# A recurrence with a mixture of experts: the shared experts' activations turned by DMA instead of TensorE

## The reference

```python
x = x + wkv(w, u, layernorm(x), ctx)        # a recurrence over the 128 tokens of each sample
n = layernorm(x)                            # (2048 tokens, 512)
p, sel = top_k(softmax(n @ gate_w.T), 2)    # 8 routed experts, two of them per token
routed = sum_e p_e * (silu(n @ G_e.T) * (n @ U_e.T)) @ D_e.T      # inner size 256
shared = (silu(n @ Gs.T) * (n @ Us.T)) @ Ds.T                     # inner size 1024
x = x + routed + sigmoid(n @ gs.T) * shared
```

## Time and profile before

| | us |
|---|---|
| time, median of 3 runs | 565.46 (563.67 to 566.19) |
| time of the profiled execution | 566.06 |
| its span, first to last instruction | 564.3 |
| TensorE busy | 486.2 (86% of the span) |
| VectorE busy | 421.3 (75%) |
| POOL busy | 345.4 (61%) |
| ScalarE busy | 275.9 (49%) |

### The profile page before, as it was taken

One profiled execution on the slowest core, in us unless ns is written; L12 is line 12 of the kernel. 1 busy time (PEld: TensorE's weight loads), 2 busy tenths in 40 slices (PEclk: granted clock), 3 DMA queues, 4 the chain that ended last, 5 costly groups with the idle time before them and its releaser, 6 DMA issues.

```text
span 564.3 us, 10142 instructions
## 1 busy us (share of the span) xinstructions
PE 486.2 (86%) x2671; PEld 258.5 (46%) x2671; DVE 421.3 (75%) x954; ACT 275.9 (49%) x534; POOL 345.4 (61%) x422
## 2 busy tenths in 40 slices
PE   1116789899999999999999979999999999999970
PEld 1113345345455555454555435445545555555530
DVE  5678987899989899999898867566656656666650
ACT  4848837575573864765837333433333333333310
POOL 5767956857948669588486364334375565555332
PEclk9999989999999999999999999999999999999995
DMA  7970105105213223151101320315576776677453
GB/s 283 415 271 19 38 19 187 57 21 188 76 46 143 77 82 143 38 188 62 52 20 39 105 88 15 113 45 102 101 122 117 141 119 116 110 131 123 69 73 38
DMA packets 25929, 59.14 MB, mean 105 GB/s; under 512 B 6314, under 2 KB 6314, under 8 KB 24338
## 3 DMA queue, kind: packets, MB, share of 16 engines
q0 software_dynamic: 9824, 20.90, 21.3%
q1 hardware_dynamic: 16050, 37.59, 18.5%
HBM read 37.83 MB, written 20.65 MB: 104 GB/s over the span
## 4 chain that ended last, share of the span: by engine, by line
PE 52%; POOL 17%; issue 10%; DVE 9%; DMA 7%; ACT 3%; SPq 1%; POOLq 0%; DVEq 0%; ACTq 0%
PE GU L884 28%; PE DN L899 14%; DMA out<-wall,idsa 5%; POOL wall L445 4%; PE XT L829 3%; PE HT L829 3%; POOL yb L429 2%; POOL nrm L411 2%; POOL nrm L413 2%; DVE wall L1071 2%; POOL wall L424 2%; POOL wall L421 2%; DVE wall L1078 1%; PE YT L829 1%; SPq L366 1%
## 5 line engine op out<-in xcount | busy, mean ns | idle before, releaser
L884 PE MATMUL GU<-wall,xt 128*128 128x512 f16 x768 | 187.0, 384 | 2.1 <-DVE wall L1173 2.0
L899 PE MATMUL DN<-wall,hx 128*128 128x512 f16 (+1 forms) x618 | 150.8, 380 | 7.2 <-DVE hx L1200 4.5
L884 PEld LDWEIGHTS GU<-wall,xt 128*128 128x128 f16 x768 | 74.8, 99 | 70.4 <-issue 3.7
L584 POOL DMA_INDIRECT out<-wall,idsa x39 | 62.0, 1590 | 73.1 <-SPq L370 35.1
L659 ACT ACTIVATE hx<-HT 128x256 f16<-128x256 f32 x103 | 39.0, 379 | 127.4 <-PE HT L829 110.6
L899 PEld LDWEIGHTS DN<-wall,hx 128*128 128x128 f16 x618 | 60.4, 98 | 81.9 <-issue 6.0
L1200 DVE TENSOR_TENSOR hx<-HT,hx 128x256 f16<-128x256 f32 x103 | 43.1, 418 | 64.3 <-ACT hx L659 59.7
L654 ACT ACTIVATE th<-GU,scl 128x256 f32<-128x256 f32 x103 | 48.5, 471 | 80.0 <-PE GU L884 76.1
L884 PE MATMUL GU<-wall,kb 128*128 x240 | 61.4, 379 | 0.2 <-DVE kb L1374 0.2
L884 PE MATMUL GU<-wall,xnb 128*128 x228 | 58.5, 379 | 0.6 <-DVE xnb L1374 0.6
L574 POOL DMA_INDIRECT xb<-xn_rows,idsi x39 | 40.2, 1030 | 30.5 <-DMA out<-xb 16.3
(11 more groups left out here) (163 smaller groups left out, 747.3 us busy)
## 6 DMA issues: line engine op xcount, KB each, us to landing
wall<-wgu SPq DMA_DIRECT2D x12, 1024.0 KB, 9.7
wall<-wd SPq DMA_DIRECT2D x12, 512.0 KB, 10.3
out<-xb SPq DMA_DIRECT2D x20, 256.0 KB
xb<-x SPq DMA_DIRECT2D x16, 256.0 KB, 2.7
cb<-ctx_t SPq DMA_DIRECT2D x16, 256.0 KB
xn_rows<-xnb SPq DMA_DIRECT2D x16, 256.0 KB
xb<-xn_rows,idsi POOLq DMA_INDIRECT x39
out<-wall,idsa POOLq DMA_INDIRECT x39
```

What stands on the lines that cost most here:

```text
L584: pool.indirect_dma_start(out, bass.IndirectOffsetOnAxis(ap=idsa[:, j:j + 1], axis=0), ye[j % RESULTS], None, compute_op=ALU.add).then_inc ...
L884: ins = nc.tensor.matmul(GU[par][:], lhs(xp, c), gate_up(base, wp, c), start=m == 0, stop=m == 3 * HC - 1)
L899: ins = nc.tensor.matmul(DN[:], hx[par][:, hp * IE + c * P:hp * IE + (c + 1) * P], down(base, wp, c), start=start and m == 0, stop=stop an ...
```

## The change

The 64 shared units' activations are no longer transposed on TensorE. `unit_hi` and `hidden_lo` now work on hb itself and leave both f16 halves in row layout in a new buffer hr (two of them); SP then issues one transposing DMA for each unit (`turn_hidden`), hr (128 x 512, f16) into hx, of which there are now three. The down products of every unit, routed ones too, come three units behind (HX = 3) instead of two. The routed units keep their transposes on TensorE, into bank YT instead of HT. The accumulate of the sums moves later in VectorE's lists: in a turn from behind hidden_lo(n) to behind hidden(n+2), likewise in the two blocks of shared units, and accumulate(15) from expert unit 1 to expert unit 2. hidden_lo(n) moves ahead of first_stats. The weights of a routed expert are loaded in six DMAs of 256 KB, spread over two turns and placed between the transposing DMAs, and some loads of x come a turn later. After the last routed unit stand its transposes and then three down products. One of the two hb buffers is now the bank HB (the former HT). Some small buffers share memory with others.

```diff
 GUW, DW = HC * 2 * IE, IC * H
 UW = GUW + DW
 LAG = 2
+HX = 3
+PIECES = 6
 NX = LAG + 1
 NB = 6
 SPLIT0 = 1
...
 
         KT, YT, XT, LG = bank("KT"), bank("YT"), bank("XT"), bank("LG")
         GU = [bank("GU0"), bank("GU1")]
-        HT, DN = bank("HT"), bank("DN")
+        HB, DN = bank("HB"), bank("DN")
+        hb = [HB[:, 0:IE], hb1[:, :]]
+        hb_routed = [by_time[:, 0:IE], hb1[:, :]]
 
 
         small_ld, x_ld, c_ld, e_ld = sems("small_ld x_ld c_ld e_ld")
...
                 sp.dma_start(xn_dram[first * P:last * P, H:XW].rearrange("(t p) e -> p t e", p=P),
                              r_d[:, first * E:last * E].rearrange("p (t e) -> p t e", e=E)).then_inc(probs_st, 16)
 
-            def load_expert(e):
-                base = (e + 1) * UW
-                wait_from(sp, e_ld, e * 32)
-                if e >= 2:
-                    sp.wait_ge(sh_gu_lo, SU)
-                    sp.wait_ge(sh_d_lo, SU)
-                src = (wgu[e], wd[e]) if isinstance(e, int) else tuple(
-                    w[ds(e, 1), :, :].rearrange("a p n -> (a p) n") for w in (wgu, wd))
-                sp.dma_start(span(wall, base, GUW), src[0]).then_inc(e_ld, 16)
-                sp.dma_start(span(wall, base + GUW, DW), src[1]).then_inc(e_ld, 16)
+            def load_expert(e, first=0, last=PIECES):
+
+                base, n = (e + 1) * UW, UW // PIECES
+                if first == 0:
+                    wait_from(sp, e_ld, e * PIECES * 16)
+                    if e >= 2:
+                        sp.wait_ge(sh_gu_lo, SU)
+                        sp.wait_ge(sh_d_lo, SU)
+                for k in range(first, last):
+                    src = wgu[e][:, k * n:(k + 1) * n] if k * n < GUW else wd[e][:, k * n - GUW:(k + 1) * n - GUW]
+                    sp.dma_start(span(wall, base + k * n, n), src).then_inc(e_ld, 16)
+
+            def turn_hidden(n):
+
+                sp.wait_ge(h_lo, n + 1)
+                wait_from(sp, dn, n - HX + 1)
+                sp.dma_start(hx[n % HX][:, :].rearrange("p (c t) -> p c t", t=P), hr[n % 2][:],
+                             transpose=True).then_inc(h_turned[n % HX], 16)
 
             sp.dma_start(wu_sb[:], wu).then_inc(small_ld, 16)
             sp.dma_start(wr_raw[:], wr).then_inc(small_ld, 16)
...
             sp.dma_start(ids_tiles[LISTS:LISTS + 1, :], pad_rows[0:1, :].bitcast(I32)).then_inc(ids_zst, 16)
             load_expert(0)
 
+            for i in range(LAG):
+                if i > 0:
+                    load_ctx(i + 1)
+                    load_expert(1)
+                    store_xn(i - 1)
+                load_x(i + 3)
+
             def turn(i, j, sq_e, hi_e, ws_e, lo_e):
-                if 0 < i < B - 1:
+                n = j * SU
+                due = squares_of(i + 1) if i + 1 in SQUARED_IN[2:] else squares_of(i + 2) if i + 2 in SQUARED_IN[2:] else None
+                k = PIECES // 2 if i + 1 in SQUARED_IN[2:] else 0
+
+                def piece(u):
+                    if due is not None:
+                        load_expert(due, k + u, k + u + 1)
+
+                if j > 0:
+                    turn_hidden(n - 1)
+                if i == LAG:
+                    load_x(i + 3)
+                if i > LAG + 1 and i + 2 < B:
+                    load_x(i + 2)
+                if i < B - 1:
                     load_ctx(i + 1)
-                if i == 1:
-                    load_expert(1)
-                if i + 1 in SQUARED_IN[2:]:
-                    load_expert(squares_of(i + 1))
-                if i > 0:
-                    store_xn(i - 1)
-                if j is not None and j > 0:
+                piece(0)
+                turn_hidden(n)
+                piece(1)
+                turn_hidden(n + 1)
+                store_xn(i - 1)
+                piece(2)
+                turn_hidden(n + 2)
+                if j > 0:
                     store_sum(j - 1)
-                if i + 3 < B:
-                    load_x(i + 3)
                 if i == B - 1:
                     store_probs(0, 0, PART)
 
-            turns(turn)
-
+            turns(turn, LAG)
+
+            n = SU * (B - LAG)
+            turn_hidden(n - 1)
             sp.wait_ge(y_rdy, B)
-            load_expert(E - 1)
+            load_expert(E - 1, 0, 3)
+            turn_hidden(n)
             store_xn(B - 1)
+            load_expert(E - 1, 3, 6)
+            turn_hidden(n + 1)
+            turn_hidden(n + 2)
             store_sum(B - LAG - 1)
 
+            turn_hidden(n + 3)
             store_probs(1, PART, B)
-            for j in range(B - LAG, B - 1):
-                store_sum(j)
+            for u in range(3):
+                turn_hidden(n + SU + u)
+            store_sum(B - 2)
+            turn_hidden(N_EXP - 1)
             store_sum(B - 1)
 
             sp.wait_ge(waits_rdy, WAIT_STEPS)
             for j in range(1, NSLOT):
-
 
                 for r in range(min(j, RESULTS)):
                     if j < RESULTS:
...
                 nc.scalar.activation(th[par][:], GU[par][:, 0:IE], ACT.Tanh, scale=scale(row, TANH)).then_inc(tanh, 1)
 
             def unit_hi(n, par):
-                act.wait_ge(h_t, n + 1)
-                wait_from(act, dn, n - 1)
-                nc.scalar.activation(hx[par][:, 0:IE], HT[:, 0:IE], ACT.Copy).then_inc(h_hi, 1)
+                if n >= N_EXP:
+
+                    act.wait_ge(h_t, n - N_EXP + 1)
+                    act.wait_ge(dn, n - HX + 1)
+                    nc.scalar.activation(hx[n % HX][:, 0:IE], YT[:, 0:IE], ACT.Copy).then_inc(h_hi, 1)
+                    return
+                act.wait_ge(h_rdy, n + 1)
+                if n >= 2:
+                    act.wait_ge(h_turned[(n - 2) % HX], 16 * ((n - 2) // HX + 1))
+                nc.scalar.activation(hr[par][:, 0:IE], hb[par], ACT.Copy).then_inc(h_hi, 1)
 
             def gu_square(s):
                 act.wait_ge(sh_ld[s], 32)
...
             unit_hi(n, 0)
             router_out(B - 1)
             unit_tanh(n + 1, 1, SHARED)
+            unit_hi(n + 1, 1)
             expert_square(E - 1, 0)
-            unit_hi(n + 1, 1)
             unit_tanh(n + 2, 0, SHARED)
             expert_square(E - 1, 1)
             expert_square(E - 1, 2)
...
                                            stop=m == 3 * HC - 1)
                 return ins
 
-            def hidden_t(n, par):
+            def hidden_t(n):
                 pe.wait_ge(h_rdy, n + 1)
-                wait_from(pe, h_lo, n)
-                transposes(HT, hb[par], IC, h_t)
-
-            def down_products(n, par, base, start, stop, sums):
-                pe.wait_ge(h_lo, n + 1)
+                pe.wait_ge(h_lo, n)
+                transposes(YT, hb_routed[n % 2], IC, h_t)
+
+            def down_products(n, base, start, stop, sums):
+                if n < N_EXP:
+                    pe.wait_ge(h_turned[n % HX], 16 * (n // HX + 1))
+                else:
+                    pe.wait_ge(h_lo, n + 1)
                 if start:
                     wait_from(pe, dn_free, sums)
                 for m in range(3 * IC):
                     c, (hp, wp) = m // 3, HI_LO[m % 3]
-                    ins = nc.tensor.matmul(DN[:], hx[par][:, hp * IE + c * P:hp * IE + (c + 1) * P],
+                    ins = nc.tensor.matmul(DN[:], hx[n % HX][:, hp * IE + c * P:hp * IE + (c + 1) * P],
                                            down(base, wp, c), start=start and m == 0, stop=stop and m == 3 * IC - 1)
                 ins.then_inc(dn, 1)
 
...
                     between()
                 products(par, lhs, base, 3, 6)
                 if before is not None:
-                    down_products(n - 2, par, *before)
-                if not (isinstance(n, int) and n == 0):
-                    hidden_t(n - 1, 1 - par)
+                    down_products(n - HX, *before)
+                if n > N_EXP:
+                    hidden_t(n - 1)
                 if beyond is not None:
                     beyond()
                 products(par, lhs, base, 6, 3 * HC).then_inc(gu, 1)
...
                 for u in range(SU):
                     if j == 0:
                         pe.wait_ge(sh_gu_lo, u + 1)
-                    if u >= 2:
-                        before = shared_down(j, u - 2)
-                    else:
-                        before = None if j == 0 else shared_down(j - 1, SU - 2 + u)
-                    if before is not None and SU * j + u - 2 < SU:
-                        pe.wait_ge(sh_d_lo, SU * j + u - 1)
+                    m = SU * j + u - HX
+                    before = shared_down(m // SU, m % SU) if m >= 0 else None
+                    if 0 <= m < SU:
+                        pe.wait_ge(sh_d_lo, m + 1)
                     unit(SU * j + u, u % 2, lhs, sh_base(u), before, between.get(u), beyond.get(u))
                     beside(u)
 
...
                 if j == 4:
 
                     pe.wait_ge(last_lo, 1)
```

(38 more changed lines are left out.)

21 lines of the change are left out of this document (12 added, 9 removed).

## The result

The changed kernel takes 614.41 us (median, 612.38 to 615.35), the kernel before 565.58: a ratio of 1.0865, 95% interval 1.0827 to 1.0903. The prediction was 582.7 with a range of 570 to 600, so the direction was right and the size far too small: 49 us lost instead of 17.

The account below looks back on a forecast made before the run. It took TensorE, busy 86% of the span, as the bound, with VectorE's chain 92% full in the mix. From the profiled 566.06 us, 566.06 + 8.8 - 0.3 + 4.1 + 4.0 = 582.7, range 570 to 600.

Parts of the forecast that it names:

- The accumulate moved on VectorE: Turns 4 to 14: down products wait 1.5 to 2.6 us a turn for the later accumulate; +8.8 us, bounds 0 and +13.
- turn 9's terms: Turn 9's loop through VectorE and ScalarE: 4.93, 6.12, 4.81, 1.55, 0.1, 2.6 and 0.2, sum 20.3 against 19.63 us.
- The transposes: Shared units: taking two transposes each off TensorE frees 0.22 us a unit, 13.8 us in all as an upper bound.
- The DMA transposes: SP queue: each takes 3 to 4 us, the issues behind have several us to spare; cost 0.
- Last blocks: Last blocks of shared units: -1.7 for transposes gone, +1.2 and +0.2 for the later accumulate; sum -0.3 us.
- Routed stage: Handover to routed experts: later last shared down product and accumulate(15) delay gather 5 and the first add; +4.1 us.
- End: End of the run: slot 36's product waits for the last hidden block, its rows come later; +4.0 us (3.5 to 5).
- C: Rival: transposing DMAs are late, over about 7 us each they stop TensorE; 615 us at 9.7 each; chance 0.13.
- B: Rival: the accumulate waits but VectorE's loop is no longer than the old turn; only the ends cost; 574 us; chance 0.17.
- D: Rival: the accumulate is not late, so 13.8 us is saved and the two ends are paid; 560 us; chance 0.08.

Follow-up runs that it names:

- e1: The changed kernel with accumulate(j-1) early again, ahead of hidden_lo(n+1) instead of behind hidden(n+2): 571.81 us, 1.0142 of the kernel before.
- e2: The changed kernel with both hb buffers in PSUM (bank HB), the late accumulate kept: 594.47 us, 1.0539 of the kernel before.
- e5: The changed kernel with the edits of e1 and e2 together, early accumulate and both hb buffers in PSUM: 571.03 us, 1.0092 of the kernel before.
- e4: The changed kernel with 12 useless products ahead of each of 13 waits for the accumulate: 600.46 us, 1.0639 of the kernel before.
- e3: The changed kernel with the shared units' transposes back on TensorE, lag and late accumulate kept: 591.02 us, 1.0451 of the kernel before.
- e7: e5 with the routed units' down products two units behind again instead of three: 562.47 us, 0.9925 of the kernel before.
- e8: e7 with each routed expert's weights loaded in two DMAs instead of six pieces: 567.19 us, 1.0018 of the kernel before.

## Why the prediction was wrong

**Mechanism right, term mis-sized.** The step that failed is "The accumulate moved on VectorE": +8.8 for turns 4 to 14, with bounds of 0 and +13. By the YT of sample 15 it measured +34.0, and undoing it brings 42.6 (e1). The place, the 15 waits and the loop through VectorE and ScalarE are as laid out; turn 9's terms agree to 0.1 in three of five. Three things were missing.

- *The subtraction from SBUF*, costed "at nothing, plus or minus 0.1 us each". It was 0.37 on the mean and 0.9 where it mattered, and the page of the Trainium skill named above ("SBUF — State Buffer") states the exclusion, without a price; I looked up the removed transposes and not the operands of the instructions that stay. Worth 20 us (e2), 17.3 of them ahead of the YT of sample 15, nearly all of it inside the loop (e5).
- *The clock*. I had the waits at 1.5 to 2.6 us and gave them no other price. They were 2.1 to 3.8, the clock fell behind some of them and stretched the 12 products in the loop. Worth some 10 us of e4's 14, and it overlaps with the 20: by the granted clock of each turn from 4 to 15 it fell in six turns here and in three of e2.
- *The early turns, and the loads behind the transposing DMAs.* e2, without the slow subtraction, still loses 16.7 us up to the YT of sample 15, where 8.8 was forecast. Some 2.6 of the difference are the clock in turns 9 and 11, and turns 4 and 5 lose 4.0 instead of 1.6. In e3, whose profiled execution is 28.5 longer, 18.2 of them by its YT rows, turns 3 to 5 lose 5.8 instead of 1.6 and turns 6 to 13 11.0 instead of 6.4; but there 1.8 is the pair of transposes in its loop, and the rest the even turns' wait for them, neither of which the changed kernel has. In the changed kernel the waits for x add 2.7. Why turns 4 and 5 lose more was not tested.

**The other steps.** The transposes: 0.22 us a unit by the spacing is right, odd turns of e1 and e5 are 0.87 shorter. The DMA transposes: taken as 3 to 4 us each, they land in 2.5, and no product waits for one; that the issues behind them have several us to spare was not so for x. The queue carries seven pieces of 256 KB in most turns, 1.75 MB and not 1.25. The 1309 ns that the Trainium skill ("VectorE: DVE Perf Modes", The three transpose paths) gives for a 128x128 block would have made 5.2 us of it, as an estimate; SP's instruction takes 1.19 for four such blocks. Last blocks -0.3: measured +2.7 in the changed kernel; not taken apart. Routed stage +4.1: measured 8.0 in the changed kernel, where other gathers wait too, and 5.4 from e5 to e7. End +4.0: measured 3.4 and 3.7.

**The rivals.** C's 615 is the measured time, by chance: no product of the changed kernel waits for a transposing DMA. B and D fall with the 13 waits of 2.1 to 3.8 us and turns 3 to 14 of over 20. D's point, an accumulate that is not late, is what e1 has, with both ends paid: it takes 571.8 and not 560, since POOL's wait takes a part of the 13.8.

## What to carry to other kernels

When a wait moves onto the last link of a loop, list that loop's every instruction with its operands: a cost of nothing holds only for what stays in the same memory, at the same time as the same neighbour. A TensorE that stands for 2.4 to 3.8 us paid twice in some of these turns, in the wait and in the clock behind it. And what work taken off a full engine brings is read from who is second: here POOL was 0.8 us behind every second turn, and took back what the even turns had saved until two scatters made way.

## What the hardware showed that I had not expected

- A VectorE subtraction of 128x256 with both operands in SBUF takes 0.36 to 0.43 us in 20 of 32 rows, 1.35 when it starts 0.19 behind POOL's 1.26 us product, and 2.2 once beside POOL's 4.21 us subtraction; with one of them in PSUM it takes 0.36 to 0.43. Moving the buffer cures it (0.79 to 0.41 on the mean, e2).
- Useless products ahead of a wait made the kernel 14 us faster (e4), some 10 of them by keeping the clock up.
- A transposing DMA of 128x512 f16 from SBUF to SBUF takes 1.19 us of its issuing engine and lands in 2.5; with the experts' loads undivided in its queue it was up to 3.7 us late for its product (e8).
